# Multi-head latent attention with a feed-forward layer on one core: joined half-width bursts and a moved product

## The reference

```python
q = rmsnorm(x @ Wq_a, w) @ Wq_b              # rank 192, then 32 heads of 128 + 64
ckv = x @ Wkv_a                              # 64 latent columns + 64 rotated ones
kv = rmsnorm(ckv[..., :64], w2) @ Wkv_b      # per head 128 keys + 128 values
scores = (q_nope @ k_nope.T + rope(q_pe) @ rope(k_pe).T) * 192 ** -0.5
probs = softmax(causal(scores))
o = concat(probs @ v over the heads) @ Wo
x = x + layernorm(o)
x = x + layernorm(ffn(layernorm(x)))
```

## Time and profile before

| | before |
|---|---|
| median of 3 runs | 637.61 us (636.57 to 638.52) |
| the profiled execution | 637.57 us, of which span 635.8 us |
| TensorE busy | 603.3 us, 95%, mean granted clock 0.991 |
| VectorE busy | 522.8 us, 82% |
| ScalarE busy | 419.0 us, 66% |
| GpSimd busy | 133.6 us, 21% |
| line 628, 64 times | mean 942 ns |
| load of `sq`, 448 KB | 3.4 us from issue to landing |
| attention pairs | from some 46 to 465 us of the span |

### The profile page before, as it was taken

The page is one execution under the profiler, slowest core; times in us unless marked ns, Lnnn a source line. Parts: engine busy times, 40 slices in busy tenths (PEclk is TensorE's granted clock), DMA queues, the critical chain, the costliest instruction groups (busy, mean ns, idle before and its releaser), DMA issues.

```text
span 635.8 us, 12431 instructions
## 1 busy us (share of the span) xinstructions
PE 603.3 (95%) x3432; PEld 446.3 (70%) x3432; DVE 522.8 (82%) x1315; ACT 419.0 (66%) x1165; POOL 133.6 (21%) x124
## 2 busy tenths in 40 slices
PE   4778999999999999999999999999999999899996
PEld 4666767777677677776777777767678888675664
DVE  5897788888888888888888888888877888889456
ACT  4456768777778787777777777878873545265343
POOL 2011122213222222222222322223000000025620
PEclk9998999999999999999999999999999999999999
DMA  8000201202112022021120220203283000001003
GB/s 318 26 1 1 84 23 62 82 0 82 38 45 82 3 79 77 6 82 37 45 82 0 82 57 25 82 29 124 84 276 145 1 1 1 29 1 51 1 16 117
DMA packets 13862, 37.80 MB, mean 59 GB/s; under 512 B 1328, under 2 KB 1584, under 8 KB 13584
## 3 DMA queue, kind: packets, MB, share of 16 engines
q1 hardware_dynamic: 13840, 37.53, 17.5%
HBM read 31.24 MB, written 6.29 MB: 59 GB/s over the span
## 4 chain that ended last, share of the span: by engine, by line
PE 77%; DVE 13%; issue 4%; ACT 3%; DMA 2%; SPq 0%; ACTq 0%; DVEq 0%
PE bank L1027 13%; PE bank L986 13%; PE bank L988 13%; PE bank L987 13%; PE bank L1039 13%; PE bank L1057 3%; PE bank L1049 2%; PE bank L996 2%; DVE dot L838 2%; PE bank L1010 2%; PE bank L1009 2%; DVE ss L638 1%; DMA sq<-sq 1%; PE bank L1204 1%; DVE st L812 1%
## 5 line engine op out<-in xcount | busy, mean ns | idle before, releaser
L362 ACT ACTIVATE pr<-ss,small 128x128 f32<-128x128 f32 (+3 forms) x256 | 143.2, 559 | 41.4 <-DVE small L638 40.7
L370 ACT ACTIVATE pt<-bank 128x128 f32<-128x128 f32 (+3 forms) x256 | 110.9, 433 | 61.2 <-PE bank L1027 60.9
L638 DVE CUSTOM_DVE_ANT_0 ss<-bank,cst 128x128 f32<-128x128 f32 (+3 forms) x256 | 123.2, 486 | 13.8 <-PE bank L988 9.5
L1027 PEld LDWEIGHTS bank<-ident,pr 128*128 128x128 f32 x640 | 75.7, 142 | 66.7 <-ACT pr L362 34.0
L1027 PE MATMUL bank<-ident,pr 128*128 128x128 f32 x640 | 119.0, 284 | 3.1 <-ACT pr L362 3.0
L286 POOL TENSOR_TENSOR qrot<-qrot,qswp 64x512 f32<-64x512 f32 x64 | 82.8, 1293 | 138.4 <-DVE qrot L624 138.4
L986 PE MATMUL bank<-kt_hi,qt_hi 128*128 128x128 f32 (+3 forms) x256 | 101.0, 394 | 3.6 <-DVE qt_lo L628 2.7
L1039 PE MATMUL bank<-pt,kvn 128*64 128x256 f32 (+3 forms) x512 | 86.2, 448 | 0.7 <-ACT pt L370 0.7
L988 PE MATMUL bank<-kt_hi,qt_lo 128*128 128x128 f32 (+3 forms) x256 | 83.3, 325 | 0.0
L987 PE MATMUL bank<-kt_lo,qt_hi 128*128 128x128 f32 (+3 forms) x256 | 83.1, 325 | 0.0
L628 DVE TENSOR_TENSOR qt_lo<-qrot,qt_hi 128x512 fp32r<-128x512 f32 x64 | 60.3, 942 | 24.6 <-ACT qt_hi L352 24.5
(11 more groups left out here) (168 smaller groups left out, 1133.2 us busy)
## 6 DMA issues: line engine op xcount, KB each, us to landing
sv<-sv SPq DMA_DIRECT2D x16, 576.0 KB, 3.7
sq<-sq SPq DMA_DIRECT2D x16, 448.0 KB, 3.4
wvo_scratch<-vs SPq DMA_DIRECT2D x16, 256.0 KB, 2.1
wv_raw<-wvo_scratch SPq DMA_DIRECT2D x8, 512.0 KB, 4.2
xa<-x SPq DMA_DIRECT2D x8, 256.0 KB, 5.9
x<-x SPq DMA_DIRECT2D x1, 2048.0 KB, 10.7
out<-yo SPq DMA_DIRECT2D x8, 256.0 KB, 2.0
w<-w SPq DMA_DIRECT2D x1, 1376.0 KB, 13.1
```

The source lines that it names most:

```text
L362: nc.scalar.activation(pr[:, k % 4, 0:n], ss[:, k % 2, 0:n], ACT.Exp, bias=negmax[:, k % 8:k % 8 + 1], scale=-1.0, accum_out=rsum[:, k:k + ...
L370: nc.scalar.activation(pt[:, b, h, 0:i + 1, i * P:(i + 1) * P], bank[2 + k % 2][:, 0:(i + 1) * P].rearrange("p (j q) -> p j q", q=P), ACT. ...
L638: nc.vector.tensor_tensor_reduce(out=ss[:, k % 2, 0:n], in0=bank[k % 2][:, 0:n], in1=mask[:, SEQ - n:SEQ], scale=-SCALE, scalar=3.4e38, op ...
L1027: last = nc.tensor.transpose(bank[2 + k % 2][:, j * P:(j + 1) * P], pr[:, k % 4, j * P:(j + 1) * P], ident[:, :])
```

## The change

On TensorE, output step 1 at k = 2 and steps 2 and 3 at k = 3 become steps 1 to 3 at k = 2. The value-output product moves from k = 8 to k = 9, directly ahead of output step 0, with its wait for the preceding contents of bank 5. On ScalarE the copy of the product to `vs` moves from k = 9 to k = 10, where it stands behind the move of the turned probabilities of unit 10, the exponent of unit 12 and the copy of a query's high part. The calls of `query` at k = 5 and 7 only move in the text. A pair then has four bursts: k = 1, 2, 9 and 10.

```diff
@@ -442,7 +442,7 @@
                         move_r(2 * p - 1)
                     if k == 12:
                         move_r(2 * p, first)
-                    if k == 9:
+                    if k == 10:
                         act.wait_ge(a.wvo_made, p + 1)
                         if not first:
                             act.wait_ge(a.wvo_out, 16 * p)
@@ -1088,24 +1088,21 @@
                     if k == 1 and not first:
                         output(2 * p - 1, 1, [0])
                     if k == 2 and not first:
-                        output(2 * p - 1, 1, [1])
-                    if k == 3 and not first:
-                        output(2 * p - 1, 1, [2, 3])
+                        output(2 * p - 1, 1, [1, 2, 3])
                     if k == 4 and not first:
                         if last:
                             pe.wait_ge(a.r_moved, 2 * p - 1)
                         else:
                             pe.wait_ge(a.wq_split, p + 2)
                         turn_r(2 * p - 1)
-                    if k == 8:
+                    if k in (5, 7) and not last:
+                        query(4 * p + 4 + k // 7, 0, k // 7, p + 1)
+                    if k == 9:
                         if first:
                             pe.wait_ge(a.wq_split, p + 2)
                         else:
                             pe.wait_ge(a.r_moved, 2 * p)
                         absorb_output(p)
-                    if k in (5, 7) and not last:
-                        query(4 * p + 4 + k // 7, 0, k // 7, p + 1)
-                    if k == 9:
                         output(2 * p, 0, [0], first)
                     if k == 10:
                         output(2 * p, 0, [1, 2, 3])
```

## The result

The changed kernel takes 665.6 us (median; 665.3 to 666.4) against 637.6 us: 1.045 times the time before, with an interval of 1.044 to 1.047. It is 28.0 us slower. Its profiled execution has a span of 664.6 us, 28.8 more than before's 635.8.

What follows compares the result with a forecast made beforehand. TensorE, busy 95% of the span, was taken to bound the kernel. To 637.6 us came 27.1, mainly waits for the moved copy, giving 664.7, plus 6.8 for clock falls: 671.5, stated as 672, range 656 to 682.

Steps and rivals of the forecast that it cites:

- The likeliest case: Whole kernel: the wait for the moved copy plus some falls of TensorE's clock, 672 us (668 to 681), chance 0.50.
- Rival (a): Whole kernel: the same wait, but TensorE's clock holds, 664.7 us (663 to 667), chance 0.27.
- The moved copy: ScalarE's copy to vs at position 10 makes TensorE wait 1.78 us before turning reciprocals; bounds 0 and 1.9 us.
- The second half's lost cover: Positions 8 to 9: without the product's cover, the mask of scores 9 holds scores 11; gain only 0.02 us a pair.
- The first half: Outputs joined at position 2: the saved 0.29 us only lengthens the wait at position 6; gain 0, bounds 0 and 4.4.
- The last pair: Last pair: changed wait for the copy, and position 8's product without cover; cost 1.0 us, bounds 0 and 1.8.
- The clock: TensorE falls to 1.2 GHz after 4 of 16 standstills, 1.7 us each: 6.8 us, bounds 0 to 27.
- Rival (c): Whole kernel: the wait comes, but the bursts' 9.0 us gain comes through too, 656 us, chance 0.09.
- rival (d): Position 11: the moved copy does not end last and the bursts pay in full, 628.6 us, chance 0.04.
- rival (e): Whole kernel: gain and wait cancel, or bursts don't join on the engine; change under 0.3%, chance 0.02.
- rival (b): Attention stage: TensorE's clock falls in nearly every pair, 692 us, chance 0.06.

Runs made afterwards that it cites:

- copy_only: The kernel before, with its six bursts, and only ScalarE's copy of the product to vs moved to position 10: 664.6 us, ratio 1.042.
- scale_late: The changed kernel with the vs copy back at position 9 and VectorE's output scaling moved from position 6 to 7, behind the mask of scores 9: 633.3 us.
- copy_back: The changed kernel with one edit undone, the copy to vs again at ScalarE's position 9: 638.2 us, ratio 1.001.
- wait_2: The changed kernel with two small ScalarE copies ahead of the moved copy, so that TensorE stands still longer: 674.9 us.
- first_join: The kernel before with only the first-half join, output steps 1 to 3 at position 2: 637.1 us, ratio 1.000.
- order_first: The kernel before with VectorE's second-head rotation behind mask and subtraction at position 3, and the first-half join alone: 629.4 us, ratio 0.988.
- both_holds_l8: The changed kernel with vs copy at position 9, VectorE's rotation and scaling later, and the last pair's product at position 8: 626.8 us, ratio 0.984.
- order_only: The kernel before, six bursts, with only VectorE's second-head rotation moved behind mask and subtraction at position 3: 630.9 us, ratio 0.991.

## Why the prediction was right, and where it was not

**The time.** 665.6 us lies in the range of 656 to 682 and on the forecast side. The likeliest case, 672 with some falls of the clock, was not what happened: it was 6.4 us too long, the 6.8 us that it put down for the clock. Rival (a), the same sum with the clock held, 664.7, was, within 1 us. The chances as they stand add up to 0.98, and the 0.94 for slower has 0.02 that no case carries.

**The moved copy: right.** Predicted: the copy starts 1.29 us behind ScalarE's move of the probabilities and TensorE stands still for 1.78 us. Measured: 238.13 - 236.84 = 1.29, and 2.20 - 0.44 = 1.76. copy_only shows that it stands alone. In the first row behind the wait there is 0.06 us more: the reciprocals take 0.50 us to the next row's start instead of 0.44; the bounds had 0.1 for this, as an unhidden weight load. With it 27.42 forecast for a pair becomes 27.48.

**The second half's lost cover: right.** Predicted: scores 11 held by the mask of scores 9 for 0.27 us, and the joined burst finishing where the two do today. Measured: scores 11 are 231.39 - 230.46 = 0.93 us behind scores 10, where 0.65 would do, so held by 0.28; from there to position 9's transposes 2.76 us against 2.74 worked out. scale_late shows that it is this mask. In the first pair, where the prediction said that nothing holds scores 11, the join gave 0.29 us, as taken.

**The first half: right in the sum, wrong in the sign to look for.** The time from scores 4 to position 6's transposes is 228.21 - 220.97 = 7.24 us, before 7.25. But I said that the wait at position 6 would grow from 0.2 to 0.5 us, and its idle is 0.19. Some 0.28 us are spent one place earlier, at scores 7: they start 0.39 us behind the transpose at 225.04, when the mask of unit 5 is done (225.35), and this doesn't show as an idle at all. A wait shorter than the modelled tail of the matmuls in front of it leaves no idle in the list; only the distance between starts tells it.

**The last pair** was to cost 1.0 us and cost 1.26: copy_only has 0.40 of it, and copy_back 0.86, the product without its cover. The prediction named both parts.

**The clock: the step that failed.** I compared 1.78 us, measured from start to start, with 1.92 and 2.03, which are idle as the row states it. On the rows' own scale the new standstill is 1.60 us. That scale does not settle the matter by itself, as 1.80 us by the idle row is also below 1.92: none of 15 pairs falls at 1.60, four do at 1.80, six at 1.99. So the four falls taken for the changed kernel, which no row fixed, came out at none; that wait_2 has just four says nothing for them. The price of a fall, 1.7 us, was about right (1.57). The trace of before had a third case, not in the earlier trace rows: idle 2.70 us up to 45.37, and half the clock from 47.1 us on for 3.4 us; it changes nothing in the argument. The Trainium skill's advice (TensorE: Matmul & The Clock Gate, Why this matters for your kernels) allowed this standstill, and there the run agrees with it; wait_2 shows falls at 1.80 us, which that advice would also allow, and there the measurement decides against it.

**Rival (c)**, the gain coming through with the wait, was refuted by copy_back and first_join; **rival (d)** by the first row of the waits, and so was **rival (e)**; **rival (b)** by the periods, of which none shows a fall.

## What to carry to other kernels

Before saving work on the busiest engine, ask at each place what the next thing to hold it is: here two holds of 0.3 us on an engine that is 95% busy ate nearly all of a saving worked out at nine microseconds, and reordering two steps on the second engine gave 6 us. When a copy that frees a buffer is moved in an in-order queue, count everything it gets behind up to the moment its waiter arrives. And compare lengths only on one scale: a stall from start to start is longer than the idle that its row states.

## What the runs showed of the hardware

- A subtraction on VectorE that starts while GpSimd adds took 1.66 us instead of 0.69; kept apart, all 64 take 0.68 to 0.71.
- TensorE's clock was granted at 1.2 GHz for 3.4 us after single standstills as short as 1.80 us by the idle row, in a stretch where it is otherwise busy throughout. It cost 1.57 to 1.58 us each time. It happened after 4, 6 and 8 of 15 equal standstills of 1.80, 1.99 and 2.36 us (the 16th is shorter in each kernel and was followed by none), in a regular order of pairs, and after none of 15 of 1.60.
- A half-width burst joined to another saved 0.29 us in the changed kernel's first pair and 0.20 us a pair in order_first. scale_late has 0.31 us a pair less than before, with the scaling moved and one of its two joins eaten, and both_holds_l8 0.27 less than order_only for two joins, where holds took the rest.
